# Modulation merged into the projection stage, and the slot table laid out partition by partition

## The chip, the cores and the metric

The kernel runs on one core of a Trainium2 chip, as one program with one launch. The metric is the device time of an execution in microseconds (us); the median of several runs counts.

## What is computed

One block of a transformer with adaptive LayerNorm: 8 batches of 1024 tokens, 512 wide. A small vector c per batch gives six rows (shift, scale and gate for each half of the block); the second half is a mixture of 32 experts with 4 experts chosen per token and room for 256 tokens each.

```python
mod = (_silu(L0_c) @ L0_wmod).reshape(L0_c.shape[0], 6, 1, -1)
sa, ca, ga, sb, cb, gb = (mod[:, 0], mod[:, 1], mod[:, 2], mod[:, 3], mod[:, 4], mod[:, 5])
ga = (2 * (ga >= 0) - 1) * jnp.maximum(jnp.abs(ga), 0.25)
gb = (2 * (gb >= 0) - 1) * jnp.maximum(jnp.abs(gb), 0.25)
h = _layernorm(x, axis=-1) * (1 + ca) + sa
x = x + ga * _L0_attn_ref(h, w_q, b_q, w_k, b_k, w_v, b_v, w_o, b_o)
h = _layernorm(x, axis=-1) * (1 + cb) + sb
x = x + gb * _L0_ffn_ref(h, gate_w, bias_corr, up_w, down_w, shared_up_w, shared_down_w)
...
pos = jnp.take_along_axis(jnp.cumsum(oh, axis=0) - 1, e_flat[:, None], axis=1)[:, 0]
valid = pos < CAP
xe = jnp.zeros((E, CAP, D), flat.dtype).at[e_flat, pos].set(flat[tok], mode='drop')
```

## The kernel before

The program is a row of five stages, each a block of its own: modulation, projection to Q, K and V, attention, the feed-forward stage (output projection, routing, shared expert), and the 32 experts. A stage begins when the one before has ended on all engines, its DMAs included. Within a stage the five engines run their own hand-written orders and meet by semaphores. Semaphores of most stages start with a credit of 16, which one engine (SP in the projection and the expert stage) gives by one increment each at the stage's start, ahead of its first DMA.

**Modulation** (lines 103 to 194) loads c and the six 1 MB parts of `wmod`, computes silu(c) on ScalarE and VectorE (DVE), multiplies with an 8-column stationary operand into six PSUM banks, makes `res` (8 rows by 6 by 512) on DVE and stores it to `mod_rows` in DRAM. An fp32 matmul shows as two records in the trace. SP also stores zeros as padding and the initial slot table: `slot_info` has 8192 slots of two numbers (token, weight). Slot = expert * 256 + place, and the table in SBUF is `info[p, n]` with slot = n * 128 + p, so that neighbours along a partition lie 1 KB apart in DRAM and each slot is a piece of 8 bytes.

**Projection** (`stage_qkv`) works in 16 units of 512 tokens (two halves of each batch). For a unit, DVE makes LayerNorm statistics and normalises (`layernorm`, L370 to L378), GpSimd multiplies by the scale row and adds the shift row (`modulate`, L311 and L313; both rows are loaded by SP as broadcasts of `mod_rows`), TensorE transposes into two PSUM banks `ps_t` (`turn`), and ScalarE and DVE split the result in a high and a low part (`turn`, `low_turned`). Then come 12 products of 12 matmuls each: n = 0 to 3 with the Q weights, 4 to 7 with K, 8 to 11 with V. Weights are split in high and low parts too (`high_weights` on ScalarE, L389 on DVE), in the opening. For n below 8 ScalarE takes `out_hi` and DVE `out_lo` (L400) from a ring of four buffers each, which come free when SP's stores have landed. The work of unit u + 1 up to its transposes lies inside unit u; transposes of k = 0 to 3 come after products 7 to 10. Every other unit, SP waits for GpSimd's `modulate` of the next unit, to reload the two rows, before it issues the unit's first store.

**Experts** load the slot table (`info`) and the gate rows gb, turn them to token numbers on DVE (L1680 on), gather tokens by them, and add each expert's result to the output with an indirect DMA. In the feed-forward stage GpSimd writes token and weight of every chosen pair into `slot_info` with 16 indirect DMAs of 128 entries per unit (L1140), at the index that DVE computes in `give_slots`.

Of the kernel before, what the change touches and what calls it, by code (L numbers as in the profile page):

```python
# [102 lines left out]
def stage_modulation(nc, cT, wmod, mod_dram, h2_dram, info_dram, out):  # L103


    with ExitStack() as ctx:
        s = Scope(nc, ctx, "mod_", credit=False)
        c_sb = s.sb("c", [P, DK, NB], FP32)
        sig = s.sb("sig", [P, DK, NB], FP32)
        silu = s.sb("silu", [P, DK, NB], FP32)  # L110
        w_sb = s.sb("w", [P, DK, 6 * D], FP32)
        res = s.sb("res", [NB, 6, D], FP32)
        sign = s.sb("sign", [NB, 2, D], FP32)
        mag = s.sb("mag", [NB, 2, D], FP32)
        ps = [s.ps(f"ps{j}", (NB, D)) for j in range(6)]
        SP_TILES = SLOTS // P
        zero = s.sb("zero", [P, D], FP32)
        pad_i = s.sb("pad_i", [P, SP_TILES], I32)
        info = s.sb("info", [P, SP_TILES, 2], FP32)
        pool_own = s.sem("pool_own")  # L120
        loaded, sig_done, silu_done = s.sem("loaded"), s.sem("sig"), s.sem("silu")
        mm, own, ready, stored = s.sem("mm"), s.sem("own"), s.sem("ready"), s.sem("stored")
        gates = (M_GA, M_GB)
        ORDER = gates + (M_SA, M_CA, M_SB, M_CB)
        w_in = s.sems("w_in", 2)
        block = ctx.enter_context(nc.Block())

        @block.sync
        def _(sp):
            sp.dma_start(c_sb[:, :, :], cT.rearrange("(k p) b -> p k b", p=P)).then_inc(loaded, 16)  # L130
            for n, j in enumerate(ORDER):
                cols = slice(j * D, (j + 1) * D)
                sp.dma_start(w_sb[:, :, cols], wmod[:, cols].rearrange("(k p) n -> p k n", p=P)).then_inc(w_in[n >= 2], 16)
            sp.wait_ge(pool_own, 2)
            for r in range(CAP // P):
                sp.dma_start(h2_dram[T + r * P:T + (r + 1) * P, :], zero[:, :]).then_inc(stored, 16)
                sp.dma_start(out[T + r * P:T + (r + 1) * P, :], zero[:, :]).then_inc(stored, 16)
            sp.dma_start(info_dram.rearrange("(n p) c -> p n c", p=P), info[:, :, :]).then_inc(stored, 16)
            sp.dma_start(mod_dram[NB:NB + 1, :, :].rearrange("b j d -> (b j) d"), zero[0:6, :]).then_inc(stored, 16)
            sp.wait_ge(ready, 1)  # L140
            sp.dma_start(mod_dram[0:NB, :, :], res[:, :, :]).then_inc(stored, 16)
            sp.wait_ge(stored, 16 * (2 * CAP // P + 3))

        @block.gpsimd
        def _(pool):
            pool.memset(zero[:, :], 0.0)
            pool.memset(info[:, :, :], 0.0)
            pool.iota(pad_i[:, :], pattern=[[0, NE], [P, CAP // P]], base=T, channel_multiplier=1).then_inc(pool_own, 1)
            pool.wait_ge(pool_own, 1)
            pool.tensor_copy(info[:, :, 0], pad_i[:, :]).then_inc(pool_own, 1)  # L150

        @block.scalar
        def _(act):
            act.wait_ge(loaded, 16)
            act.activation(sig[:, :, :], c_sb[:, :, :], ACT.Sigmoid).then_inc(sig_done, 1)

        @block.tensor
        def _(pe):
            pe.wait_ge(silu_done, 1)
            for n, j in enumerate(ORDER):  # L160
                pe.wait_ge(w_in[n >= 2], (64 if n >= 2 else 32))
                for k in range(DK):
                    last = pe.matmul(ps[j][:, :], silu[:, k, :], w_sb[:, k, j * D:(j + 1) * D],
                                     start=k == 0, stop=k == DK - 1)
                last.then_inc(mm, 1)

        @block.vector
        def _(dve):
            dve.wait_ge(sig_done, 1)
            dve.tensor_tensor(silu[:, :, :], c_sb[:, :, :], sig[:, :, :], ALU.mult).then_inc(silu_done, 1)  # L170
            for n, j in enumerate(gates):
                dve.wait_ge(mm, n + 1)
                last = dve.tensor_copy(res[:, j, :], ps[j][:, :])
            last.then_inc(own, 1)
            dve.wait_ge(own, 1)

            for n, j in enumerate(gates):
                dve.tensor_scalar(sign[:, n, :], res[:, j, :], 0.0, 2.0, ALU.is_ge, ALU.mult)
                last = dve.tensor_scalar(mag[:, n, :], res[:, j, :], -1.0, 0.25, ALU.mult, ALU.max)
            last.then_inc(own, 1)  # L180
            dve.wait_ge(own, 2)
            for n, j in enumerate(gates):
                last = dve.tensor_tensor(mag[:, n, :], mag[:, n, :], res[:, j, :], ALU.max)
            last.then_inc(own, 1)
            dve.wait_ge(own, 3)
            for n, j in enumerate(gates):
# [1645 lines left out]
```

## Time and profile before

| what | value |
|---|---|
| median of 3 runs | 3338.03 us (3325.95 to 3339.06) |
| the profiled execution, its own time | 3321.04 us |
| its span | 3319.3 us |
| mean granted TensorE clock | 0.954 of full |
| busy: PE, DVE, POOL, ACT | 91%, 65%, 57%, 42% |

PE is TensorE, PEld its weight loads, DVE VectorE, ACT ScalarE, POOL GpSimd, SP the engine that issues most DMAs; SPq is its queue, where the time beside a DMA is that of issuing it. Each row of a timeline gives start, length, engine, line of the kernel, operation, output and inputs, and in brackets how long the engine had been idle and what released it.

### The profile page before, as it was taken

The numbers are of one execution on the slowest core, as the hardware profiler recorded it, in microseconds if no ns is written. First come the engines' busy times: TensorE is split into PE (matmuls) and PEld (weight loads), VectorE is DVE, ScalarE is ACT, GpSimd is POOL, SyncE is SP. The second block draws the span as 40 slices with busy tenths as digits, with TensorE's granted clock in tenths as the row PEclk, the third lists the DMA queues.
The fourth block names the chain that finished last, engine by engine and source line by source line (L and its number), as shares of the span: only waits on it lengthen the run. The fifth ranks groups of instructions, "written<-read, shape, count | busy, mean of one in ns | idle before, by whom it ended". The sixth has DMA issues, their size and how long they took to land. (4 is left out here: it accounts for less than half of the span.)

```text
span 3319.3 us, 52119 instructions
## 1 busy us (share of the span) xinstructions
PE 3023.0 (91%) x16704; PEld 2188.1 (66%) x16704; DVE 2144.3 (65%) x5331; ACT 1384.5 (42%) x2755; POOL 1888.6 (57%) x1107
## 2 busy tenths in 40 slices
PE   3999999789999999999999669999999999966997
PEld 0888888655556556555656258777777777745776
DVE  3545555377767776777677257778777777735674
ACT  1212222136666666566666432332332233214674
POOL 2332332237777777777777525565664765653664
PEclk7999999979999999999999789999999999977998
DMA  8556555555445544554453323323323223107996
GB/s 163 172 173 209 180 199 174 160 123 129 111 105 127 131 105 105 129 129 104 111 129 79 100 81 111 102 67 98 114 67 98 89 92 92 60 13 214 236 241 132
DMA packets 297669, 419.49 MB, mean 126 GB/s; under 512 B 64776, under 2 KB 148744, under 8 KB 297495
## 3 DMA queue, kind: packets, MB, share of 16 engines
q1 hardware_dynamic: 274974, 383.70, 41.9%
q0 software_dynamic: 22528, 33.72, 5.2%
q8 instruction: 86, 1.41, 0.2%
q14 instruction: 81, 0.66, 0.1%
HBM read 262.85 MB, written 153.01 MB: 125 GB/s over the span
## 5 line engine op out<-in xcount | busy, mean ns | idle before, releaser
L677 POOL TENSOR_TENSOR att_pt<-att_pt 128x2048 f32<-128x2048 f32 (+3 forms) x286 | 892.2, 3120 | 319.2 <-PE att_ps_o L825 306.0
L718 ACT ACTIVATE att_pt<-att_ps_p 128x512 f32<-128x512 f32 (+3 forms) x1536 | 679.7, 496 | 491.8 <-PE att_ps_p L874 291.9
L751 DVE CUSTOM_DVE_ANT_0 att_ps_s<-att_ps_s,att_causal 128x512 f32<-128x512 f32 (+3 forms) x1024 | 492.8, 505 | 152.4 <-PE att_ps_s L815 148.8
L871 PE MATMUL att_ps_p<-att_qs,att_ks 98*128 98x512 f32 (+3 forms) x1536 | 555.3, 386 | 6.7 <-DMA att_qs<-att_m_lo 3.2
L815 PE MATMUL att_ps_s<-att_ks,att_qs 96*128 96x512 f32 (+3 forms) x1536 | 487.9, 375 | 22.7 <-DMA att_ks<-qk_parts 22.0
L871 PEld LDWEIGHTS att_ps_p<-att_qs,att_ks 98*128 98x128 f32 x1536 | 288.9, 190 | 280.3 <-ACT att_pt L718 172.9
L757 DVE TENSOR_REDUCE att_lower<-att_ps_s 128x1 f32<-128x512 f32 x512 | 352.0, 688 | 178.7 <-PE att_ps_s L815 176.9
L1140 POOL DMA_INDIRECT slot_info<-ffn_info,ffn_slot x256 | 272.8, 1065 | 123.9 <-issue 77.6
L815 PEld LDWEIGHTS att_ps_s<-att_ks,att_qs 96*128 96x128 f32 x1536 | 278.1, 194 | 76.0 <-issue 22.4
L825 PE MATMUL att_ps_o<-att_pt,att_vs 128*32 128x512 f32 (+3 forms) x3072 | 328.0, 499 | 0.0
L311 POOL TENSOR_TENSOR qkv_x<-qkv_x,qkv_mod 128x512 f32<-128x512 f32 x64 | 91.1, 1424 | 363.6 <-DVE qkv_x L378 363.6
L1104 POOL TENSOR_TENSOR ffn_h<-ffn_h,ffn_mod 128x512 f32<-128x512 f32 x48 | 75.1, 1564 | 301.9 <-DVE ffn_h L1258 301.9
L874 PE MATMUL att_ps_p<-att_mask_k,att_ident_r 128*128 128x128 f32 x1024 | 240.1, 238 | 0.0
L1422 PE MATMUL ffn_ps_m<-ffn_dn_hi,ffn_a_hi 128*128 128x512 f32 x512 | 210.1, 410 | 9.1 <-DVE ffn_a_lo L1383 6.1
L400 DVE SCALAR_TENSOR_TENSOR qkv_out_lo<-qkv_ps_m,qkv_bqk,qkv_out_hi 128x512 fp32r<-128x512 f32 x128 | 93.4, 746 | 178.3 <-ACT qkv_out_hi L355 178.3
L1422 PE MATMUL ffn_ps_m<-ffn_dn_hi,ffn_a_lo 128*128 128x512 f32 x512 | 204.7, 400 | 2.4 <-issue 2.4
L1422 PE MATMUL ffn_ps_m<-ffn_dn_lo,ffn_a_hi 128*128 128x512 f32 x512 | 205.2, 401 | 1.3 <-issue 1.2
L1422 PE MATMUL ffn_ps_m<-ffn_hT_hi,ffn_up_hi 128*128 128x512 f32 x512 | 202.3, 395 | 3.3 <-issue 3.2
L1422 PE MATMUL ffn_ps_m<-ffn_hT_lo,ffn_up_hi 128*128 128x512 f32 x512 | 200.4, 391 | 3.6 <-issue 3.6
L1422 PE MATMUL ffn_ps_m<-ffn_hT_hi,ffn_up_lo 128*128 128x512 f32 x512 | 200.6, 392 | 2.7 <-issue 2.6
L443 PE MATMUL qkv_ps_m<-qkv_hT_hi,qkv_w_hi 128*128 128x512 f32 x512 | 200.5, 392 | 1.5 <-DVE qkv_hT_lo L383 1.5
L443 PE MATMUL qkv_ps_m<-qkv_hT_lo,qkv_w_hi 128*128 128x512 f32 x512 | 200.2, 391 | 0.0
(263 smaller groups left out, 6229.3 us busy)
## 6 DMA issues: line engine op xcount, KB each, us to landing
att_qs<-qk_parts SPq DMA_DIRECT2D x96, 512.0 KB, 6.8
att_ks<-qk_parts SPq DMA_DIRECT2D x96, 512.0 KB, 13.2
qk_parts<-qkv_out_hi SPq DMA_DIRECT2D x128, 256.0 KB, 2.6
qk_parts<-qkv_out_lo SPq DMA_DIRECT2D x128, 256.0 KB, 2.9
qkv_x<-x SPq DMA_DIRECT2D x16, 1024.0 KB, 5.5
v_rows<-qkv_out_v SPq DMA_DIRECT2D x64, 256.0 KB, 2.3
att_vs<-v_rows SPq DMA_DIRECT2D x32, 512.0 KB, 16.0
o_parts<-att_o SPq DMA_DIRECT2D x64, 256.0 KB, 6.6
```

The source lines that it names most:

```text
L400: dve.scalar_tensor_tensor(out_lo[n % RING][:, :], ps_m[n % BANKS][:, :], bqk_sb[:, n:n + 1], raw(out_hi[n % RING][:, :]), op0=ALU.add, op ...
L443: last = pe.matmul(ps_m[n % BANKS][:, :], w_part[:, k, (n % NG) * P:(n % NG + 1) * P], h_part[:, k, :], start=k == 0 and a + c == 0, stop= ...
L677: pool.tensor_tensor(into, into, tile(c)[:, :, col:UNIT], ALU.add).then_inc(add_done, 1)
L718: act.activation(tile(c)[:, h, col:UNIT], ps_p[n % NP][:, col:UNIT], ACT.Exp, scale=float(HD) ** -0.5).then_inc(exp_done, 1)
L751: dve.tensor_tensor_reduce(bank, bank, causal[:, UNIT - (c1 - c0):UNIT], scale=1.0, scalar=MASKED, op0=ALU.add, op1=ALU.max, accum_out=row ...
L757: dve.reduce_max(lower[:, low:low + 1], bank, axis=AX.X).then_inc(max_done, 1)
L815: pe.matmul(ps_s[at % NS][:, 0:c1 - c0], qs[cur.slot][0:STACK, h, t * P:(t + 1) * P], ks[cur.slot][0:STACK, h, c0:c1], start=True, stop=Tr ...
L825: last = pe.matmul(ps_o[h * HD:(h + 1) * HD, col:UNIT], vs[group.slot][:, kt, h * HD:(h + 1) * HD], tile(c)[:, h, col:UNIT], start=kt == 0 ...
L871: last = pe.matmul(ps_p[n % NP][:, col:UNIT], ks[prev.slot][:, h, kt * P:(kt + 1) * P], qs[prev.slot][:, h, q0:(qh + 1) * UNIT], start=Tru ...
L874: last = pe.matmul(ps_p[n % NP][:, col:col + P], ident_r[:, :], mask_k[:, :], start=False, stop=True)
L1140: pool.indirect_dma_start(info_dram[:, :], bass.IndirectOffsetOnAxis(slot[half][:, j:j + 1].bitcast(U32), 0), info[half][:, j, :], None, b ...
L1422: last = pe.matmul(bank, a[m], c[n], start=i + j == 0, stop=i + 1 == len(pairs) and j == 2)
```

## The change

The modulation stage is gone and its work stands in `stage_modulate_qkv`. Batch 0 takes its scale and shift rows straight from PSUM: silu of its c is copied over 128 columns (`silu_first`), so that the product has the row in all 128 partitions, and DVE, not GpSimd, multiplies and adds in unit 0. The other rows come in three pairs (`PAIRS`), each product with 32 columns (`silu_lane`), two side by side in one PSUM bank, one pair in the opening, one after product 6 of unit 0, one after product 4 of unit 1. The gate pair has five DVE operations. Weights are split in another order: Q before the transposes, K and V after. The first two units are written out, ahead of the loop. Padding is stored from the projection stage.

The slot table's SBUF layout stays `info[p, n]`, but in DRAM slot = p * 64 + n, 512 bytes in a row for each partition, and `give_slots` computes that index. In the projection and the expert stage the credits are given by TensorE, not SP.

```diff
-def stage_qkv(nc, x, wqkvT, bqk, bv, mod_dram, qk_dram, v_dram):
+def stage_modulate_qkv(nc, x, cT, wmod, wqkvT, bqk, bv, mod_dram, qk_dram, v_dram, h2_dram, info_dram, out):
...
+        PAIRS = ((M_CA, M_SA), (M_GA, M_GB), (M_CB, M_SB))
...
+        PAIR_AT = (6, 4)
...
 # SP
+            sp.dma_start(c_sb[:, :, :], cT.rearrange("(k p) b -> p k b", p=P)).then_inc(c_in, 16)
             load_x(0, 0)
-            load_mod(0)
+            load_pair(0)
...
+            sp.wait_ge(pair_done, 1)
+            load_pair(1)
+            store_rows(0)
+            sp.wait_ge(pool_own, CREDIT + 4)
+            for r in range(CAP // P):
+                sp.dma_start(h2_dram[T + r * P:T + (r + 1) * P, :], zero[:, :]).then_inc(padded, 16)
+                sp.dma_start(out[T + r * P:T + (r + 1) * P, :], zero[:, :]).then_inc(padded, 16)
+            sp.dma_start(info_dram.rearrange("(p n) c -> p n c", p=P), info[:, :, :]).then_inc(padded, 16)
...
+                if isinstance(u, int) and u == 0:
+                    sp.wait_ge(pair_done, 2)
+                    load_pair(2)
+                    store_rows(1)
...
 # DVE
+            def take_pair(n, bank):
+                dve.wait_ge(pair_done, n + 1)
+                if n == 1:
+                    dve.tensor_copy(rows[n][:, :], bank)
+                    dve.drain()
+                    dve.tensor_scalar(sign[:, :], rows[n][:, :], 0.0, 2.0, ALU.is_ge, ALU.mult)
+                    dve.tensor_scalar(mag[:, :], rows[n][:, :], -1.0, 0.25, ALU.mult, ALU.max)
+                    dve.drain()
+                    dve.tensor_tensor(mag[:, :], mag[:, :], rows[n][:, :], ALU.max)
+                    dve.drain()
+                    dve.scalar_tensor_tensor(rows[n][:, :], sign[:, :], -1.0, mag[:, :], op0=ALU.add, op1=ALU.mult).then_inc(rows_done, 1)
+                else:
+                    dve.tensor_scalar_add(rows[n][0:LANE, :], bank[0:LANE, :], 1.0)
+                    dve.tensor_copy(rows[n][LANE:2 * LANE, :], bank[LANE:2 * LANE, :]).then_inc(rows_done, 1)
...
             layernorm(0, 0, 0)
-            for j in range(3):
+            dve.wait_ge(first_done, 1)
+            dve.tensor_scalar_add(mod[:, 1, :], ps_m[0][:, :], 1.0)
...
+                if isinstance(u, int) and u < 2 and n == PAIR_AT[u]:
+                    take_pair(u + 1, ps_t[1][0:2 * LANE, :])
...
 # TensorE
+            s.give_credit(pe)
+            def pair(n, bank):
+                for i in range(2):
+                    pe.wait_ge(wmod_in[i], 16 * (n + 1))
+                for k in range(DK):
+                    for i in range(2):
+                        last = pe.matmul(bank[i * LANE:(i + 1) * LANE, :], silu_lane[:, k, :, :].rearrange("p r b -> p (r b)"),
+                                         w_mod[:, k, i, :], start=k == 0, stop=k == DK - 1)
+                last.then_inc(pair_done, 1)
...
+                if isinstance(u, int) and 0 < u < 3 and k == 1:
+                    pe.wait_ge(rows_done, u + 1)
...
+                    if isinstance(u, int) and u < 2 and n == PAIR_AT[u]:
+                        pe.wait_ge(lo_done, CREDIT + DK * (u + 1))
+                        pair(u + 1, ps_t[1])
...
 # give_slots, feed-forward stage, DVE
-                dve.tensor_scalar(over[:, :, :], place[:, :, :], float(CAP), float(SLOTS), ALU.is_ge, ALU.mult)
-                dve.scalar_tensor_tensor(place[:, :, :], expert[:, :, :], float(CAP), place[:, :, :], op0=ALU.mult, op1=ALU.add)
+                dve.tensor_scalar(over[:, :, :], place[:, :, :], float(P), float(1 - SLOTS), ALU.is_ge, ALU.mult)
+                dve.scalar_tensor_tensor(place[:, :, :], expert[:, :, :], 1.0 / NE, place[:, :, :], op0=ALU.mult, op1=ALU.add)
                 dve.drain()
-                dve.tensor_tensor(slot[half][:, :].rearrange("p (t k) -> p t k", t=UT), place[:, :, :], over[:, :, :], ALU.add).then_inc(slot_done, 1)
+                dve.scalar_tensor_tensor(slot[half][:, :].rearrange("p (t k) -> p t k", t=UT), place[:, :, :], float(SLOTS // P),
+                                         over[:, :, :], op0=ALU.mult, op1=ALU.add).then_inc(slot_done, 1)
...
 # expert stage, SP (and s.give_credit(pe) at the head of TensorE's part)
-            s.give_credit(sp)
-            sp.dma_start(info[:, :, :], info_dram.rearrange("(n p) c -> p n c", p=P)).then_inc(consts, 16)
+            sp.dma_start(info[:, :, :], info_dram.rearrange("(p n) c -> p n c", p=P)).then_inc(consts, 16)
```

SP's queue, before: from the store of the slot table in the modulation stage to the weights in the projection stage (L259 is x of unit 0, L263 the two broadcast rows; ahead of this piece stand c, the six parts of `wmod` and the padding).

```order
L138 DMA slot_info<-mod_info 128x64x2
L139 DMA mod_rows<-mod_zero 6x512
L141 DMA mod_rows<-mod_res 8x3072
L106 UNCONDITIONAL_BRANCH
L254 UNCONDITIONAL_BRANCH
L259 DMA qkv_x<-x 128x4x512
L263 DMA qkv_mod<-mod_rows 128x512 x2
L268 DMA qkv_wraw<-wqkvT 128x4x512 x3
```

The same place now, from the first load to the first pair's rows; `qkv_w_mod` holds two parts of `wmod`, and there is no end of a stage in between.

```order
L200 DMA qkv_c<-cT 128x4x8
L185 DMA qkv_x<-x 128x4x512
L193 DMA qkv_w_mod<-wmod 128x4x512 x2
L204 DMA qkv_wraw<-wqkvT 128x4x512 x3
L205 DMA qkv_bqk<-bqk 128x8
L206 DMA qkv_bv<-bv 128x512
L185 DMA qkv_x<-x 128x4x512
L193 DMA qkv_w_mod<-wmod 128x4x512 x2
L198 DMA mod_rows<-qkv_rows 8x512 x2
```

x has moved ahead of all of `wmod` but c, four parts of `wmod` have moved behind the weights, and the slot table behind the first pair's rows.

DVE's opening of the projection stage, before, from the end of `inverse_root` of unit 0 on.

```order
L97 TENSOR_SCALAR qkv_tmp<-qkv_tmp 128x4
L99 TENSOR_TENSOR qkv_rstd<-qkv_rstd,qkv_tmp 128x4
L378 TENSOR_SCALAR qkv_x<-qkv_x,qkv_mv,qkv_rstd 128x512 x4
L389 TENSOR_TENSOR qkv_w_lo<-qkv_wraw,qkv_w_hi 128x2048 x3
L383 TENSOR_TENSOR qkv_hT_lo<-qkv_ps_t,qkv_hT_hi 128x512 x4
```

And now: `qkv_mod` are the rows in all partitions, L365 is the low part of a weight, L360 and L361 take a pair.

```order
L339 TENSOR_SCALAR qkv_x<-qkv_x,qkv_mv,qkv_rstd 128x512 x4
L374 TENSOR_SCALAR qkv_mod<-qkv_ps_m 128x512
L378 TENSOR_TENSOR qkv_x<-qkv_x,qkv_mod 128x512 x4
L365 TENSOR_TENSOR qkv_w_lo<-qkv_wraw,qkv_w_hi 128x2048
L381 COPY qkv_mod<-qkv_ps_m 128x512
L385 TENSOR_TENSOR qkv_x<-qkv_x,qkv_mod 128x512 x4
L344 TENSOR_TENSOR qkv_hT_lo<-qkv_ps_t,qkv_hT_hi 128x512 x4
L360 TENSOR_SCALAR qkv_rows<-qkv_ps_m 32x512
L361 COPY qkv_rows<-qkv_ps_m 32x512
L365 TENSOR_TENSOR qkv_w_lo<-qkv_wraw,qkv_w_hi 128x2048 x2
L331 BN_STATS qkv_stats<-qkv_x 128x6 x4
```

The multiplications and additions of unit 0 have come to DVE, one weight part stands between them, and two weight parts and the first pair's rows stand behind the transposes, ahead of the statistics of unit 1 (the last row).

DVE in unit 0 now, from the first seven low outputs on; before, the eighth `qkv_out_lo` followed the seventh at once.

```order
L399 SCALAR_TENSOR_TENSOR qkv_out_lo<-qkv_ps_m,qkv_bqk,qkv_out_hi 128x512 x7
L351 COPY qkv_rows<-qkv_ps_t 64x512
L353 TENSOR_SCALAR qkv_sign<-qkv_rows 64x512
L354 TENSOR_SCALAR qkv_mag<-qkv_rows 64x512
L356 TENSOR_TENSOR qkv_mag<-qkv_mag,qkv_rows 64x512
L358 SCALAR_TENSOR_TENSOR qkv_rows<-qkv_sign,qkv_mag 64x512
L399 SCALAR_TENSOR_TENSOR qkv_out_lo<-qkv_ps_m,qkv_bqk,qkv_out_hi 128x512
L344 TENSOR_TENSOR qkv_hT_lo<-qkv_ps_t,qkv_hT_hi 128x512
```

Five operations for the gate rows (L351 to L358) have come between the seventh and the eighth low output.

## Rows read from the trace of the kernel before

**Rows 1.** The page's busy times: engine, busy us (share), instructions.
```profile
PE 3023.0 (91%) x16704; PEld 2188.1 (66%) x16704; DVE 2144.3 (65%) x5331; ACT 1384.5 (42%) x2755; POOL 1888.6 (57%) x1107
```

**Rows 2.** The chain that ended last: start us, us, what.
```profile
3076.23 5.22 DMA out<-exp_y,exp_tok_add
```

**Rows 3.** Stretches: busy us of each engine, granted clock, DMA share, GB/s.
```profile
9.40:19.20 9.80, 9.71 (x16) 1.66 (x16) 0.68 (x1) 0.00 (x0) 0.00 (x0) 1.00 1.05 404
...
34.00:42.00 8.00, 0.00 (x0) 0.00 (x0) 0.24 (x1) 0.00 (x0) 0.00 (x0) 0.80 1.14 16
...
39.00:40.00 1.00, 0.00 (x0) 0.00 (x0) 0.00 (x0) 0.00 (x0) 0.00 (x0) 0.50 0.71 16
...
90.00:92.00 2.00, 2.00 (x10) 1.65 (x9) 2.00 (x2) 0.57 (x1) 1.92 (x2) 1.00 0.00 0
```

**Rows 4.** Timeline of the modulation stage: start us, us, engine, line, operation.
```profile
9.46 9.71 PE L163 MATMUL mod_ps<-mod_w,mod_silu 128*8 128x512 f32 x16 [9.46 <-DMA mod_w<-wmod]
...
14.12 21.64 SPq L139 DMA_DIRECT2D mod_rows<-mod_zero  x1
...
15.77 0.68 DVE L173 COPY mod_res<-mod_ps 8x512 f32<-8x512 f32 x1 [12.57 <-PE mod_ps L163]
...
19.62 13.90 PE L163 MATMUL mod_ps<-mod_w,mod_silu 128*8 128x512 f32 x32 [0.46 <-DMA mod_w<-wmod]
...
35.80 0.28 SPq L141 DMA_DIRECT2D mod_rows<-mod_res  x1
```

**Rows 5.** Who waited for whom, SP, 0 to 60 us: total, times, longest.
```profile
SPq L106 <- DMA mod_rows<-mod_res: 12.5, 1, 12.5
```

**Rows 6.** Timeline of the projection stage's opening.
```profile
56.17 2.47 DVE L370 BATCH_NORM_STATS2 qkv_stats<-qkv_x 128x6 f32<-128x512 f32 x4 [21.93 <-DMA qkv_x<-x]
...
60.82 3.82 DVE L378 TENSOR_SCALAR qkv_x<-qkv_x,qkv_mv,qkv_rstd 128x512 f32<-128x512 f32 x4
...
64.56 9.90 DVE L389 TENSOR_TENSOR qkv_w_lo<-qkv_wraw,qkv_w_hi 128x2048 fp32r<-128x2048 f32 x3
...
72.39 3.19 POOL L313 TENSOR_TENSOR qkv_x<-qkv_x,qkv_mod 128x512 f32<-128x512 f32 x1
...
78.23 1.94 PE L419 MATMUL qkv_ps_t<-qkv_ident,qkv_x 128*128 128x128 f32 x8 [44.71 <-POOL qkv_x L313]
...
84.26 0.79 PE L443 MATMUL qkv_ps_m<-qkv_hT_hi,qkv_w_hi 128*128 128x512 f32 x1 [1.50 <-DVE qkv_hT_lo L383]
```

**Rows 7.** Timeline of the expert stage's opening, and the DMA row of the load of c.
```profile
2999.08 0.20 POOL L199 MEMSET exp_ident<- 128x128 f32 x1 [10.85 <-POOLq L897]
...
3000.96 0.37 SPq L1586 DMA_DIRECT2D exp_info<-slot_info  x1
...
3007.59 0.20 DVE L1680 CAST exp_tok_all<-exp_info 128x64 int32<-128x64 f32 x1 [13.37 <-DMA exp_gb<-mod_rows]
...
3012.38 1.23 DVE L1711 TENSOR_TENSOR exp_up_lo<-exp_upr,exp_up_hi 128x1024 fp32r<-128x1024 f32 x1 [3.08 <-ACT exp_up_hi L1649]
...
mod_c<-cT SPq DMA_DIRECT2D x1, 16.0 KB, 1.9
```

**Rows 8.** Timeline of the projection stage's first unit (DVE, GpSimd, SP).
```profile
84.04 2.46 DVE L370 BATCH_NORM_STATS2 qkv_stats<-qkv_x 128x6 f32<-128x512 f32 x4
...
99.00 1.30 POOL L313 TENSOR_TENSOR qkv_x<-qkv_x,qkv_mod 128x512 f32<-128x512 f32 x1
...
101.67 0.37 SPq L287 DMA_DIRECT2D qk_parts<-qkv_out_hi  x1
...
107.21 0.75 DVE L400 SCALAR_TENSOR_TENSOR qkv_out_lo<-qkv_ps_m,qkv_bqk,qkv_out_hi 128x512 fp32r<-128x512 f32 x1 [7.57 <-ACT qkv_out_hi L355]
...
121.84 0.69 DVE L407 TENSOR_TENSOR qkv_out_v<-qkv_ps_m,qkv_bv 128x512 f32<-128x512 f32 x1 [1.45 <-PE qkv_ps_m L447]
```

**Rows 9.** The page's costliest groups: busy us, mean ns, idle before.
```profile
L825 PE MATMUL att_ps_o<-att_pt,att_vs 128*32 128x512 f32 (+3 forms) x3072 | 328.0, 499 | 0.0
```

**Rows 10.** Timeline of GpSimd in the feed-forward stage, after 16 scatters.
```profile
2635.30 1.50 POOL L1104 TENSOR_TENSOR ffn_h<-ffn_h,ffn_mod 128x512 f32<-128x512 f32 x1 [15.71 <-DVE ffn_h L1258]
```

More of the change, by code:

```diff
@@ L100, in inverse_root @@
     dve.wait_ge(own, base + 5)
[L103 to L186, printed above, removed]
-                dve.scalar_tensor_tensor(res[:, j, :], sign[:, n, :], -1.0, mag[:, n, :], op0=ALU.add, op1=ALU.mult)
-            for n, j in enumerate(ORDER[2:]):
-                dve.wait_ge(mm, n + 3)
-                if j in (M_CA, M_CB):
-                    last = dve.tensor_scalar_add(res[:, j, :], ps[j][:, :], 1.0)
-                else:
-                    last = dve.tensor_copy(res[:, j, :], ps[j][:, :])
-            last.then_inc(ready, 1)
@@ L229, in stage_qkv @@
         out_v = [s.sb(f"out_v{n}", [P, D], FP32) for n in range(UT)]
+        c_sb = s.sb("c", [P, DK, NB], FP32)
+        sig = s.sb("sig", [P, DK, NB], FP32)
+        silu = s.sb("silu", [P, DK, NB], FP32)
+        LANE = 32
+        silu_lane = s.sb("silu_lane", [P, DK, LANE // NB, NB], FP32)
+        silu_first = s.sb("silu_first", [P, DK, P], FP32)
+        PAIRS = ((M_CA, M_SA), (M_GA, M_GB), (M_CB, M_SB))
+        w_mod = s.sb("w_mod", [P, DK, 2, D], FP32)
+        rows = [s.sb(f"rows{n}", [2 * LANE, D], FP32) for n in range(3)]
+        sign, mag = s.sb("sign", [2 * LANE, D], FP32), s.sb("mag", [2 * LANE, D], FP32)
+        SP_TILES = SLOTS // P
+        zero = s.sb("zero", [P, D], FP32)
+        pad_i = s.sb("pad_i", [P, SP_TILES], I32)
+        info = s.sb("info", [P, SP_TILES, 2], FP32)
         ps_t = [s.ps(f"ps_t{n}") for n in range(2)]
         ps_m = [s.ps(f"ps_m{n}") for n in range(BANKS)]
+        c_in, sig_done, silu_done = (s.sem(n, False) for n in ("c_in", "sig", "silu"))
+        wmod_in, first_done, pair_done = s.sems("wmod_in", 2, False), s.sem("first", False), s.sem("pair", False)
+        rows_done, rows_out = s.sem("rows", False), s.sem("rows_out", False)
+        padded = s.sem("padded", False)
         w_in, w_hi_done, w_lo_done = s.sems("w_in", 3), s.sem("w_hi_done"), s.sem("w_lo_done")
@@ L246, in steps @@
         def steps(eng, body):
-            with eng.Fori(0, LAST) as b:
+            for half in range(HALVES):
+                body(0, half, True)
+            with eng.Fori(1, LAST) as b:
                 for half in range(HALVES):
@@ new lines, in _ @@
+            layernorm(0, 0, 0)
+            dve.wait_ge(first_done, 1)
+            dve.tensor_scalar_add(mod[:, 1, :], ps_m[0][:, :], 1.0)
+            dve.drain()
+            for t in range(UT):
+                xt = x_sb[0][:, t, :]
+                dve.tensor_tensor(xt, xt, mod[:, 1, :], ALU.mult).then_inc(mul_done, 1)
+            low_weights(0)
+            dve.wait_ge(first_done, 2)
+            dve.tensor_copy(mod[:, 0, :], ps_m[1][:, :])
+            dve.drain()
+            for t in range(UT):
+                xt = x_sb[0][:, t, :]
+                dve.tensor_tensor(xt, xt, mod[:, 0, :], ALU.add).then_inc(h_done, 1)
@@ L412, in _ @@
         def _(pe):
+            s.give_credit(pe)
[7 more added lines that the diff above has]
+                last.then_inc(pair_done, 1)
+            pe.wait_ge(silu_done, 1)
+            for i in range(2):
+                pe.wait_ge(wmod_in[i], 16)
+                for k in range(DK):
+                    last = pe.matmul(ps_m[i][:, :], silu_first[:, k, :], w_mod[:, k, i, :], start=k == 0, stop=k == DK - 1)
+                last.then_inc(first_done, 1)
+            pair(0, ps_m[2])
             pe.wait_ge(pool_own, CREDIT + 2)
@@ L972, in stage_project_route_shared @@
         LAST = NB - 1
+        assert CAP == 2 * P
         PT = UT - 1
```

50 lines of the change are left out of this document (41 added, 9 removed).

## The prediction

> **What bounds the kernel now.** I read the page first: TensorE is busy 91% of the span [rows 1], so time can be won only where it idles. The chain that ended last shows one such place: from 3076 us to the end it is a row of 28 scatter-adds, each waiting for the one before (the first stands in [rows 2]), so whatever starts the expert stage earlier ends the kernel earlier by as much. The stretches show the other place, the start. Between 34 and 42 us next to nothing runs on any engine, while the 16 DMA engines are full and move 16 GB/s [rows 3]. The timeline says with what: SP is stuck for 21.64 us behind the store of the 64 KB slot table, which is cut in 8-byte pieces, and can issue the store of the modulation rows only at 35.80 [rows 4]; SP then waits 12.5 us for that store [rows 5]. The projection stage starts only behind that, and its first projection matmul stands at 84.26 [rows 6]. The load of the slot table and of gb keeps the expert stage from 3000.96 to 3007.59 [rows 7].
>
> The profiled execution took 3321.0 us, 1.7 more than its span. It is the fastest seen; the runs give 3326 to 3339, median 3338.0. I sum against the execution and carry the difference over to the median.
>
> **The opening, step by step.** One block replaces two, so SP issues c, x, the first two wmod parts (scale, shift), then the three weights, on one queue. In front of the scale part stand as many bytes as in front of the second gate part now, so it lands when TensorE could start before, 9.46 [rows 4]. x lands one megabyte earlier, 2.6 us at the 404 GB/s these loads reach [rows 3], at 6.9; statistics and normalising take 60.82 + 3.82 - 56.17 = 8.5 [rows 6], so x is ready at 15.4. The scale product is four fp32 matmuls, as the first gate is now, whose copy starts at 15.77 [rows 4]. That ends last. DVE then has in order, with 0.7 for a 128x512 operation (the 0.69 of [rows 8]): scale from PSUM 0.7, four multiplications 2.8, the low part of the Q weights, the shift copy 0.7, four additions 2.8.
>
> The Q weights' low part takes 9.90 / 3 = 3.3 now [rows 6]; the 128x1024 form takes 1.23 [rows 7], so twice that, 2.5, is what it costs alone. I take 2.5, since GpSimd, whose own additions grow to 3.19 beside it [rows 6] against 1.30 later [rows 8], has nothing to do in the new opening. The Trainium skill (SBUF — State Buffer, "Who interferes with whom") says that a DVE instruction with two SBUF inputs contends with a GpSimd one that reads SBUF, and the trace agrees with 3.3 and 3.19 side by side. Without that rule the opening would come out 0.8 later and the first unit 1.7 more.
>
> So h is ready at 15.8 + 0.7 + 2.8 + 2.5 + 0.7 + 2.8 = 25.3. From the first transpose to the first projection matmul it is 84.26 - 78.23 = 6.0 [rows 6], so that matmul comes at 31.3 and not 84.26: **-53.0**. The shift product and the first pair end by 23 and hide behind DVE. Bounds: at the full clock the transposes take some 1 less and the first 12 matmuls 2.5 less; TensorE's granted clock had fallen to 0.50, the 1.2 GHz level, by 39, after its last modulation matmul at 33.5 [rows 3, 4], and was at 1.00, 2.4 GHz, from 90 on, 6 us into the projection [rows 3]. In the new order it idles only about 2 us before the transposes. I leave the clock as it was (sum: 0, or -3.5). The other way, loads later by 2 and the 3.3 above: +3.
>
> **What moves into the first two units.** The two pairs left are 16 matmul records each, 32 columns wide, two lanes. A record of 512 columns is 0.43 at 2.4 GHz (13.90 / 32, the second modulation burst [rows 4]), so one by one a pair costs 6.9. The attention's 32-column matmuls take 328.0 / 3072 = 0.107 each with four lanes [rows 9], so lanes do overlap; I take two at a time, **+3.5 twice**, with 6.9 twice as the other bound. The Trainium skill (TensorEngine Tiling (Array Packing), "Key Properties") states that tiles operate in parallel and that a change of tiling mode drains the array; the trace agrees on the first, and no row here prices the second.
>
> In unit 0 there is a new wait too. DVE makes two weight parts and a pair's rows after its low transposes, 1.4 + 2.5 + 2.5 = 6.4, so it starts the next LayerNorm 6.3 after the first matmul, where it starts 0.2 before it now [rows 8]. From there GpSimd needs 16.3 (99.00 + 1.30 - 84.04) and SP, whose stores are queued behind a wait for it, issues the first store 1.4 later; the fifth low output follows 5.5 after (107.21 - 101.67) [rows 8]. Counted from the first matmul: 6.3 + 16.3 + 1.4 + 5.5 = 29.5 instead of 22.9. The ring of four output buffers thus makes DVE's seventh low output end at 32.9, and only then come the gate rows in DVE's order, five operations of 0.4 to 0.7 with three drains, 3.0: done at 35.9. TensorE must not write that bank with the second transposes until then. It reaches them at 28.0 (now: 121.84 less three steps of 3.2, less 84.26) plus 3.5 = 31.5. So it waits **+4.4**; bounds 0 (if DVE catches up) and 8. Unit 1 has no such queue: SP there waits for no GpSimd, the last pair's load (2 MB) is issued 1.4 into the unit and lands by some 10, against a need at 13.7.
>
> The padding stores stand behind SP's prologue and nobody waits for them before the end of the stage: 0. In 512-byte pieces the slot table no longer fills the queue. The routing edit puts one DVE operation for another of the same size: 0.
>
> **The expert stage.** SP loses its credit increments, so its first load goes out at about 2999.1, when the stage's first instruction runs, and not at 3000.96, and the table arrives in 128 pieces. The other small load, c, took 1.9 to land [rows 7]; with some 0.5 for a second issue info and gb are there at about 3001.6, by when TensorE has given the credits: **-6.0**, bounds -4 and -6.5. Expert weights are issued earlier by the same amount, so nothing else takes the wait's place, and the chain behind shifts as a whole [rows 2].
>
> **Sum.** -53.0 + 3.5 + 3.5 + 4.4 - 6.0 = -47.6, that is 3273.4 for a profiled execution. The median of before less that is 3290.4. As the runs before spread over 13 us with the fastest at 3326, I put the median a little lower, at **3288**.
>
> **The rivals.**
> 1. *The opening comes, but half is given back in the first two units.* Lanes don't overlap (+7), the wait is 8 (+3.6), loads land later (+3), only 4 from the expert stage (+2): 3273.4 + 15.6 = 3289 profiled, 3304 as median. For it: TensorE is the bound there and each added microsecond counts. Against: [rows 9]. Chance 0.17.
> 2. *The full clock from the start*: -3.5, and no wait in unit 0 because the stores keep up, -4.4: 3280 as median. For it: the short idle. Against: the transposes from 78.23 on did not bring the clock up before the projection began [rows 3, 6]. Chance 0.15.
> 3. *The table was not what delayed the expert stage*: with the gb rows or the weights landing last, the 6.0 is lost and the median is 3294. Chance 0.08.
> 4. *Slower.* The new index puts the 128 entries of each of the 256 scatters 512 bytes apart instead of side by side within an expert. If each took d longer on GpSimd, its 16 scatters per unit first eat the idle 15.7 that it has before its next work [rows 10], 0.98 each; from there each microsecond lands on 15 units. To cancel 48 they must take 0.98 + 48 / (15 x 16) = 1.18 longer, more than double; 1.4 longer would give 3390. Against: GpSimd only makes 128 descriptors each time, as before, and the landings are waited for a whole unit later. Chance 0.02.
> 5. *Under 0.5% in all*: an unseen wait of 30 in the unrolled code or in the merged stage's queue, 3321. Chance 0.03.
>
> The forecast itself has 0.55, with a range of its own from 3276 to 3300. A difference of 0.5% (17 us) is about what a measurement of this kernel can tell from none. Rivals 1 to 3 and the forecast are all beyond it, 0.95; same 0.03; slower 0.02. The range for 8 in 10 takes in rivals 2 and 3 and most of 1: 3268 to 3304.
>
> **What the new profile would show.** The first transposes at about 25 and the first projection matmul at 31, no stretch with full DMA engines and no bytes; scale product's end at 15.8; three DVE weight parts of 2.5 and not 3.3; TensorE waiting near 63 to 67 us for DVE's gate rows; pair records at half their length apart; the third unit's first matmul some 42 us earlier than now; SP's info load issued with the stage's start, and the first DVE cast of tokens 2.5 after it. I am wrong if scatters take over 2 us each, if TensorE waits in unit 0 for over 8, or if the expert stage still opens on a wait of 5 or more.

## The result: 0.6% faster, where 1.5% was forecast

The changed kernel takes 3315.64 us (median of 22 runs, 3299.85 to 3339.43) beside 3335.68 for the kernel before (22 runs): ratio 0.9943, 95% interval 0.9925 to 0.9961. That is 20 us less, where the prediction had 50 less than its median of 3338, and it lies outside the range of 3268 to 3304. The profiled execution took 3308.46 us, 12.6 us less in span (3306.7 against 3319.3). One repeat of the changed kernel in the last group of runs below took 8454.88 us at a granted clock of 0.35 and is left out of that kernel's ratio.

First the page of the changed kernel, the busy row that answers to [rows 1].

```profile
span 3306.7 us, 51930 instructions
PE 3024.1 (91%) x16720; PEld 2188.0 (66%) x16720; DVE 2139.4 (65%) x5338; ACT 1384.9 (42%) x2755; POOL 1873.8 (57%) x1099
```

It does not tell where the missing 30 us went: TensorE's sum is 1 us larger than before. So I read the timeline at places that both kernels have. The opening, which answers to [rows 4] and [rows 6] (start us, us, engine, line, operation):

```profile
7.06 2.47 DVE L331 BATCH_NORM_STATS2 qkv_stats<-qkv_x 128x6 f32<-128x512 f32 x4 [3.17 <-DMA qkv_x<-x]
...
9.88 9.63 PE L429 MATMUL qkv_ps_m<-qkv_w_mod,qkv_silu_first 128*128 128x512 f32 x16 [9.88 <-DMA qkv_w_mod<-wmod]
...
16.12 0.69 DVE L374 TENSOR_SCALAR qkv_mod<-qkv_ps_m 128x512 f32<-128x512 f32 x1 [2.48 <-PE qkv_ps_m L429]
...
19.30 2.29 DVE L365 TENSOR_TENSOR qkv_w_lo<-qkv_wraw,qkv_w_hi 128x2048 fp32r<-128x2048 f32 x1
19.44 3.63 PE L421 MATMUL qkv_ps_m<-qkv_w_mod,qkv_silu_lane 128*32 128x512 f32 x16
...
24.86 1.06 PE L440 MATMUL qkv_ps_t<-qkv_ident,qkv_x 128*128 128x128 f32 x8 [1.79 <-issue]
...
29.63 0.50 PE L466 MATMUL qkv_ps_m<-qkv_hT_hi,qkv_w_hi 128*128 128x512 f32 x1 [1.41 <-DVE qkv_hT_lo L344]
```

Each step stands within half a microsecond of where the prediction put it, until the transposes, which run at a granted clock of 1.00: 1.06 us for the first eight where it was 1.94 [rows 6]. The expert stage's opening, which answers to [rows 7]:

```profile
2990.53 0.35 SPq L1613 DMA_DIRECT2D exp_info<-slot_info  x1
2990.53 0.21 POOL L105 MEMSET exp_ident<- 128x128 f32 x1 [10.05 <-POOLq L923]
...
2993.50 0.20 DVE L1707 CAST exp_tok_all<-exp_info 128x64 int32<-128x64 f32 x1 [7.77 <-DMA exp_gb<-mod_rows]
```

The load goes out with the stage's first instruction and the cast follows 2.97 later. Now the marks side by side, each a start time read from the timeline:

| mark | before | after | difference |
|---|---|---|---|
| fourth LayerNorm of the projection | 157.01 | 115.81 | -41.2 |
| feed-forward stage, first ffn_h of VectorE | 1923.55 | 1883.61 | -39.9 |
| expert stage, GpSimd's first instruction | 2999.08 | 2990.53 | -8.6 |
| first transpose of the expert stage | 3017.10 | 3003.51 | -13.6 |
| end of the span | 3319.3 | 3306.7 | -12.6 |

The opening's gain arrives at the feed-forward stage almost whole, and 31.4 of it is gone when that stage ends. The change alters three small operations in that stage, of the same sizes as before. Its units show the pattern: before the change, units follow each other in about 63.2 us; after it about every second one takes 69.6. The two windows are one such unit of each (busy us of PE, PEld, DVE, ACT, POOL with counts, granted clock, DMA share, GB/s), before and then after:

```profile
2571.70:2634.70 63.00, 60.52 (x283) 48.93 (x282) 48.82 (x103) 19.52 (x34) 40.26 (x34) 0.97 0.27 88
```

```profile
2143.10:2212.70 69.60, 61.32 (x275) 47.99 (x274) 47.96 (x103) 19.64 (x34) 39.25 (x34) 0.95 0.23 76
```

No engine has more work. TensorE's 61.32 us instead of 60.52 go with a granted clock of 0.95 instead of 0.97; the rest of the 6.6 us is waiting. VectorE's timeline of the changed kernel inside such a unit shows on what:

```profile
2168.05 0.18 DVE L1388 SCALAR_TENSOR_TENSOR ffn_slot<-ffn_place,ffn_over 128x16 int32<-128x16 f32 x1
2174.16 0.29 DVE L1407 TENSOR_TENSOR ffn_logits<-ffn_logits,ffn_ps_g 128x128 f32<-128x128 f32 x1 [5.93 <-issue]
...
2176.62 0.23 DVE L1311 TENSOR_TENSOR ffn_pair_hi<-ffn_biased 128x64 f32<-128x64 f32 x1 [1.37 <-issue]
```

L1388 is the last operation of the loop's body and L1407 the first: the 5.93 us lie across the jump back. L1311, a few operations on, waits a second time, 1.37 us; experiments e9 to e12 come back to it. "Issue" means that the engine waited for nothing that the profile shows: no semaphore, no buffer. What ended VectorE's idle time before that sum of logits, before the change and after it (us, times):

```profile
L1379 DVE TENSOR_TENSOR ffn_logits<-ffn_logits,ffn_ps_g x16: 286/289/291, 1948.8 to 2907.9; 128x128 f32<-128x128 f32 x16
...
  issue: 1.8, 5
```

```profile
L1407 DVE TENSOR_TENSOR ffn_logits<-ffn_logits,ffn_ps_g x16: 286/289/289, 1908.6 to 2899.7; 128x128 f32<-128x128 f32 x16
...
  issue: 30.4, 5
```

Five times 6 us, once for each jump back of a loop with six passes. The page's part on queues shows what went on meanwhile. These are the queues that load instructions (packets, MB, share), before and after.

```profile
q8 instruction: 86, 1.41, 0.2%
q14 instruction: 81, 0.66, 0.1%
```

```profile
q8 instruction: 89, 1.46, 0.2%
q14 instruction: 107, 0.88, 0.1%
```

26 more packets of 8 KB (0.88 MB in 107). By windows, 25 of them fall into 1880 to 3000 us. One pass of the loop after the change, from 2249 to 2382, has this row; the same window of the kernel before, 2251 to 2378, has none at all:

```profile
q14 instruction: 5, 0.04, 0.1%
```

Over all five passes behind a jump (2168.2 to 2839.2) the changed kernel has 25 packets on q14 and one on q8; the kernel before (2213.4 to 2849.4) has one on q8 and none on q14:

```profile
q14 instruction: 25, 0.20, 0.1%
q8 instruction: 1, 0.02, 0.0%
```

### The profile page after: what moved, and what is told of

Read it like the earlier page. It is cut to its first block and busy times, and to the rows that moved or that the text cites. A ratio compares the mean times of both kernels' runs of the same rounds, so it can differ in the third digit from the quotient of the medians.

```text
span 3306.7 us, 51930 instructions
## 1 busy us (share of the span) xinstructions
PE 3024.1 (91%) x16720; PEld 2188.0 (66%) x16720; DVE 2139.4 (65%) x5338; ACT 1384.9 (42%) x2755; POOL 1873.8 (57%) x1099
## 3 DMA queue, kind: packets, MB, share of 16 engines
q8 instruction: 89, 1.46, 0.2%
## 5 line engine op out<-in xcount | busy, mean ns | idle before, releaser
L1167 POOL DMA_INDIRECT slot_info<-ffn_info,ffn_slot x256 | 269.4, 1052 | 123.4 <-issue 77.3
L271 POOL TENSOR_TENSOR qkv_x<-qkv_x,qkv_mod 128x512 f32<-128x512 f32 x60 | 83.5, 1392 | 385.0 <-DVE qkv_x L339 385.0
L900 PEld LDWEIGHTS att_ps_p<-att_mask_k,att_ident_r 128*128 128x128 f32 x1024 | 196.3, 192 | 5.7
```

Source lines behind the costliest of these rows:

```text
L900: last = pe.matmul(ps_p[n % NP][:, col:col + P], ident_r[:, :], mask_k[:, :], start=False, stop=True)
L1167: pool.indirect_dma_start(info_dram[:, :], bass.IndirectOffsetOnAxis(slot[half][:, j:j + 1].bitcast(U32), 0), info[half][:, j, :], None, b ...
```

## Theories

**A: the code's place.** Counted in the built program, VectorE's loop of the feed-forward stage is some 349 instructions of 64 bytes (to within two). A packet of 8 KB is a block of 128 instructions, so the loop is 2.7 packets long. The merged opening is unrolled and puts 88 more instructions ahead of it: it began at 4482, 2 past a multiple of 128, and now at 4570, 90 past. The theory: if the loop touches 3 blocks they stay with the engine; if 4, each jump back fetches the code anew. **B: the scatter.** The table's new index makes something in the stage slower. **C: another engine's code**, ScalarE's (35 later) or TensorE's (711 later), sets the stall and VectorE only shows it.

The kernel before took a median of 3325, 3239 and 3305 us in the three groups of runs below (e1 to e5; e6, e3, e7, e8; e9 to e12), so kernels are compared within a group.

## Experiments

### e1_pad40: VectorE's loop 40 instructions later

```diff
         def _(dve):
+            for _ in range(40):
+                dve.drain()
             dve.wait_ge(iotas, CREDIT + 1)
```

> The changed kernel with 40 drains ahead of VectorE's first wait of the feed-forward stage, where it stands idle 7.22 us for a load. Counted in the built program, VectorE's loop of that stage is 349 instructions of 64 bytes and begins at instruction 4482 before the change and at 4570 after it (88 later); in blocks of 128 (the 8 KB of an instruction packet) it touched 3 blocks before and touches 4 after. The drains put it at 4610, where it touches 3 again. Theory A (each jump back to the loop's start makes VectorE's code be fetched anew when it touches 4 blocks): instruction packets of the 8 KB queue fall from 107 to about 83, the feed-forward stage from 995 us back to 963, the whole by about 31, to a profiled time near 3277 and 0.982 to 0.986 of the kernel before. Theory B (the new slots' scatter holds up the stage): no change, 3308, 0.994. Theory C (it is the code of ScalarE or TensorE that moved): no change, 3308.

A drain computes nothing. The 40 of them stand in front of the stage's first wait and delay nothing: the first ffn_h starts at 1883.52 with them and at 1883.61 without.

Measured: 3280.63 us against 3324.57 before, ratio 0.9852 (0.9807 to 0.9897). Packets and VectorE's idle time before the sum of logits:

```profile
q14 instruction: 82, 0.67, 0.1%
```

```profile
L1409 DVE TENSOR_TENSOR ffn_logits<-ffn_logits,ffn_ps_g x16: 286/289/289, 1909.2 to 2873.2; 128x128 f32<-128x128 f32 x16
...
  issue: 1.6, 5
```

And the stage as a window, from its first ffn_h to its last, without the drains and with them:

```profile
1883.61:2882.00 998.39, 916.38 (x4179) 729.65 (x4180) 713.99 (x1476) 298.49 (x515) 571.90 (x482) 0.96 0.28 88
```

```profile
1883.52:2855.48 971.96, 907.05 (x4179) 728.68 (x4180) 715.78 (x1476) 298.15 (x515) 575.63 (x482) 0.97 0.29 90
```

The 40 drains take 26.4 us off the stage. TensorE, too, is busy 9 us less for the same matmuls: its granted clock over the stage is 0.97 and was 0.96. B and C predicted no change and are out as the main cause.

### e2_before88: the same stall put into the kernel before

```diff
         def _(dve):
+            for _ in range(88):
+                dve.drain()
             dve.wait_ge(iotas, CREDIT + 1)
```

> The kernel before with 88 drains at the same place and nothing else, so that VectorE's loop of the feed-forward stage begins at 4570, as in the changed kernel. Theory A: slower by about 31 us (1.009 of the kernel before), some 24 more 8 KB instruction packets, all of it in the feed-forward stage, with idle times of about 6 us ahead of VectorE's sum of logits in five iterations. Theories B and C: no change but for what the drains themselves take beyond the idle time (under 1 us).

Measured: 3354.05 us, ratio 1.0085 (1.0052 to 1.0118): 29.5 slower, with nothing of the change in it.

```profile
q14 instruction: 106, 0.87, 0.1%
```

```profile
L1381 DVE TENSOR_TENSOR ffn_logits<-ffn_logits,ffn_ps_g x16: 286/288/290, 1944.5 to 2938.8; 128x128 f32<-128x128 f32 x16
...
  issue: 29.9, 5
```

25 more packets than the kernel before and the same five stops. A loss of the size of the changed kernel's (31.4) follows from the place of the code alone.

### e4_act93 and e5_old_table: ScalarE's code, and the table

```diff
+            for _ in range(93):
+                act.drain()
             high_weights(0, NW_UP)
```

> The changed kernel with 93 drains ahead of ScalarE's first wait of the feed-forward stage (idle 17.64 us there), so that ScalarE's loop stands 128 instructions after its place in the kernel before, that is the same within a block. Theory C for ScalarE: the stage falls to 963 us and the time to near 3277. Theory A: no change, 3308, and 107 instruction packets as before.

Measured: 3307.11 us (one run), 107 packets, five stops with 30.2 us. C for ScalarE is out. TensorE's code had no run of its own, but in e1 and e2 it stayed where it was while the stall went and came, and q8, the queue whose bytes fit TensorE's code, loads one packet in the five passes with the stall and one without.

```diff
-            sp.dma_start(info[:, :, :], info_dram.rearrange("(p n) c -> p n c", p=P)).then_inc(consts, 16)
+            sp.dma_start(info[:, :, :], info_dram.rearrange("(n p) c -> p n c", p=P)).then_inc(consts, 16)
...
-                dve.tensor_scalar(over[:, :, :], place[:, :, :], float(P), float(1 - SLOTS), ALU.is_ge, ALU.mult)
-                dve.scalar_tensor_tensor(place[:, :, :], expert[:, :, :], 1.0 / NE, place[:, :, :], op0=ALU.mult, op1=ALU.add)
+                dve.tensor_scalar(over[:, :, :], place[:, :, :], float(CAP), float(SLOTS), ALU.is_ge, ALU.mult)
+                dve.scalar_tensor_tensor(place[:, :, :], expert[:, :, :], float(CAP), place[:, :, :], op0=ALU.mult, op1=ALU.add)
```

The padding's store and the last line of the index go back in the same way.

> The changed kernel with the slot table and the scatter's index as before the change; the merged opening stays and VectorE's count of instructions is the same. Theory B (the scatter's new addresses hold up the feed-forward stage): the stage falls from 995 us towards 963, the time to about 3277 plus the 6 to 11 us that the expert stage's opening gives back. Theory A: the stage stays at 995, and the expert stage's opening gives back its 6 to 11 us, so 3314 to 3320.

Measured: 3325.71 us (one run), 107 packets: the stall stays, so B is out. Against the changed kernel's 3306.7 the span is 17.2 longer, and the loss is not where I expected most of it. SP's timeline in the merged opening, with the old table and then with the new:

```profile
33.23 0.46 SPq L215 DMA_DIRECT2D slot_info<-qkv_info  x1
33.73 16.23 SPq L216 DMA_DIRECT2D mod_rows<-qkv_zero  x1
50.01 1.37 SPq L185 DMA_DIRECT2D qkv_x<-x  x1
```

```profile
34.66 0.46 SPq L215 DMA_DIRECT2D slot_info<-qkv_info  x1
35.16 0.36 SPq L216 DMA_DIRECT2D mod_rows<-qkv_zero  x1
35.57 0.39 SPq L185 DMA_DIRECT2D qkv_x<-x  x1
```

The store in 8-byte pieces holds SP for 16.23 us, now in the middle of the first unit, whose outputs wait behind it: the fourth LayerNorm comes at 124.78 and not 115.81, +9.0. In the expert stage the cast of the tokens comes 7.1 after GpSimd's first instruction (3006.84 to 3013.98) and not 2.97, +4.2. The remaining 4 us lie in the feed-forward stage and at the end; it is one execution, and no cause is shown for them.

### e6_table_only: the second part of the change alone

```diff
-            sp.dma_start(info_dram.rearrange("(n p) c -> p n c", p=P), info[:, :, :]).then_inc(stored, 16)
+            sp.dma_start(info_dram.rearrange("(p n) c -> p n c", p=P), info[:, :, :]).then_inc(stored, 16)
...
-                dve.tensor_scalar(over[:, :, :], place[:, :, :], float(CAP), float(SLOTS), ALU.is_ge, ALU.mult)
+                dve.tensor_scalar(over[:, :, :], place[:, :, :], float(P), float(1 - SLOTS), ALU.is_ge, ALU.mult)
```

> The kernel before with the second part of the change alone: the slot table laid out partition by partition and the index to match; the modulation stage stays. VectorE's loop stays at 4482, so theory A expects no loss in the feed-forward stage (967 us). The store of the padding table (8 B pieces, behind which SyncE's next issue took 21.64 us and whose stage ended at about 50 us) no longer holds the stage up: some 12 us less; the expert stage's opening, from its load of the table to its first transpose, takes 12.5 to 13 us and not 16.1. Sum about -15, ratio near 0.9955. If the table's layout were worth nothing ahead of the merged opening, -3.5 alone, 0.999.

Measured: 3225.56 us against 3239.45, ratio 0.9955 (0.9941 to 0.9968); the first projection matmul at 72.72 where it was 84.26 [rows 6]. 80 packets, no stops. So the table alone is worth 14 us in the old order and, by the one run of e5, some 13 to 17 in the new.

### e3_pad128, e7_pad64, e8_pad84: is it the drains or the place?

```diff
-            for _ in range(40):
+            for _ in range(128):
                 dve.drain()
```

With 64 and 84 in the other two.

> The changed kernel with 128 drains at the same place as the 40 that gave 27 us back: VectorE's loop stands at 4698, one block of 128 later than in the changed kernel, and touches 4 blocks again. Theory A: 107 instruction packets on the 8 KB queue and the feed-forward stage at about 998 us, 3307 to 3310 in all. Rival (the drains themselves, or their pause, are what helps): about 3281.

> 64 drains: the loop is at instructions 4634 to 4981, in blocks 36 to 38, so 3 blocks. Theory A with blocks of 128 counted from the program's start: 82 instruction packets, stage near 972 us, time near 3281.

> 84 drains: the loop is at instructions 4654 to 5001, in blocks 36 to 39, so 4 blocks, with 20 more instructions ahead of it than with 64. Theory A: 105 to 107 packets, stage near 998 us, time near 3308.

Measured, with 3239.45 for the kernel before and one run each: 3220.31 us and 108 packets with 128 drains, 3214.94 and 107 with 64, 3210.89 and 108 with 84. All three stall, five times 6.1 to 6.2 us. Packets and stops came out as expected for 128 and 84 drains; the times that were expected were those of the first group. 64 was expected to be free of the stall and is not, so blocks counted from the program's own first instruction are wrong. The control matters most: 128 drains move the code by one whole block, and cure nothing. In this group a pass of the loop (two units) took 118.5 us without a stall (e6) and 122.4 to 123.7 with it (mean of five), so the same 6 us of VectorE cost 4 to 5; in the two profiles of the result it took 127.2 before the change and 134.2 after it, 7 more.

### e9_after_again, e10_pad40_again, e11_pad24, e12_pad52: the limits, and the better kernel

e9 is the changed kernel and e10 is e1, both unaltered; e11 and e12 have 24 and 52 drains.

```diff
-            for _ in range(40):
+            for _ in range(24):
                 dve.drain()
```

> The changed kernel, unaltered, beside the next three on one chip, since the runs with 64, 84 and 128 drains came from a session in which the kernel before took 3239 us and not 3325. Theory A: 107 instruction packets, ratio to the kernel before 0.991 to 0.995, five idle times of about 6 us ahead of VectorE's sum of logits.

> The 40 drains again, now beside the changed kernel: 82 packets, none of the five idle times, and faster than the changed kernel by the whole of what they cost, 20 to 31 us by the session: ratio to the kernel before 0.984 to 0.988.

> 24 drains: the loop at 4594 to 4941. The runs so far bear theory A out but not the count from the program's start: 4482 and 4610 (2 past a multiple of 128) let the loop stay, 4570 and 4698 (90 past), 4654 (46 past) and 4634 (26 past) don't. A loop of 349 stays within 3 blocks from 36 starts of 128, so something of 10 to 33 instructions must stand ahead of the program in the chip. 4594 is 114 past (14 short of the next multiple): it stays if that is 14 or more (82 packets), and does not if it is 10 to 13 (107).

> 52 drains: the loop at 4622, 14 past a multiple of 128. By the same count it stays (82 packets, no idle times) if 10 to 21 instructions stand ahead of the program, and does not (107) if it is 22 to 33. If it is the drains' own time and not the place that counts, it is as good as with 40.

| kernel | loop starts at | past 128 | packets | stops' sum, us | time (before 3304.70) |
|---|---|---|---|---|---|
| e9, no drains | 4570 | 90 | 107 | 30.7 | 3290.91, 0.9946 (0.9927 to 0.9965) |
| e11, 24 | 4594 | 114 | 82 | 1.7 | 3246.84 (one run) |
| e10, 40 | 4610 | 2 | 83 | 1.6 | 3249.73, 0.9830 (0.9804 to 0.9856) |
| e12, 52 | 4622 | 14 | 107 | 31.6 | 3276.89 (one run) |

The twelve drains between e10 and e12 bring the five stops back, those between e11 and e10 don't matter. With a loop of 349 that must lie within 3 blocks of 128, starts 114 and 2 are good and 14, 26, 46 and 90 bad only if 22 to 33 instructions stand ahead of the program on the chip.

The start times of the packets, read from the trace, show the blocks in another way. In e12 the pass behind the jump at 2419.4 loads packets at 2423.8, 2426.3, 2451.9, 2499.3 and 2548.8. Packets in 2419.5 to 2430, 2430 to 2465, 2465 to 2510 and 2545 to 2551:

```profile
q14 instruction: 2, 0.02, 0.5%
...
q14 instruction: 1, 0.01, 0.1%
...
q14 instruction: 1, 0.01, 0.1%
...
q14 instruction: 1, 0.01, 0.3%
```

Two come at the jump. The other three come when 84, 216 and 342 of VectorE's instructions of the pass have started, which is 98, 102 and 100 past a multiple of 128; in e7 it is 99, 101 and 96. So a block ends near there, which puts some 26 to 32 instructions ahead of the program, and on entering a block the engine loads the one behind it. That explains the count: a loop that touches 4 blocks also loads a fifth, which it never runs, and one that touches 3 loads a fourth. Four blocks stay and five do not. This is inferred from the packets' times; no row shows what the engine holds.

The second, small wait in the changed kernel fits this too. From a start at 90 only a dozen instructions are left in the first block, and L1311 behind them waits 6.4 us in all, six times; in e12 and e7, which start at 14 and 26, it does not wait.

The 40 drains beat the kernel before in both of their groups and the changed kernel in the one where both were timed. There they are 1.2 points below it, 41 us, more than the 31 of VectorE's stops. The five passes behind a jump show why, as windows of the kernel before and after, of e10 and e9, and of e6 and e7 (another kernel each, but the same feed-forward stage), each time without and with the stall (columns as in the windows above):

```profile
2213.40:2849.40 636.00, 604.77 (x2823) 486.32 (x2822) 484.08 (x1021) 195.70 (x340) 403.83 (x340) 0.99 0.29 91
2168.20:2839.20 671.00, 618.48 (x2821) 490.31 (x2820) 481.64 (x1021) 196.12 (x340) 398.64 (x340) 0.97 0.28 86
...
2164.90:2789.00 624.10, 602.53 (x2822) 485.17 (x2821) 484.81 (x1021) 196.03 (x340) 402.23 (x340) 0.99 0.30 93
2179.20:2840.20 661.00, 617.21 (x2822) 489.82 (x2821) 481.66 (x1021) 196.20 (x340) 395.76 (x340) 0.97 0.28 88
...
2189.40:2782.00 592.60, 592.60 (x2822) 481.62 (x2821) 485.58 (x1021) 195.21 (x340) 402.99 (x340) 1.00 0.31 98
2158.70:2773.00 614.30, 602.57 (x2822) 486.64 (x2821) 483.73 (x1021) 195.74 (x340) 399.03 (x340) 0.99 0.30 94
```

With the stops of 30 us TensorE idles 21, 22 and 12 us longer (window less its busy time), and the same matmuls take 14, 15 and 10 us longer. The granted clock reads 0.50, the 1.2 GHz level, for 44, 41 and 17 us of these windows, and for 17, 14 and 0 us without the stall. One such place in the changed kernel: TensorE idles 4.0 of 7.4 us, and then the clock is down:

```profile
2315.00:2322.40 7.40, 3.43 (x13) 2.13 (x12) 3.70 (x18) 1.64 (x3) 5.57 (x7) 1.00 0.02 0
2322.40:2329.10 6.70, 5.57 (x12) 3.75 (x12) 3.75 (x9) 3.45 (x7) 0.32 (x1) 0.50 0.00 0
```

Other pairs give less: 24 us between e4 and e1 (668.8 and 645.3), 26 between e12 and e10 (649.9 and 624.1). What sets the cost within 22 to 37 us is not shown. Of the 55 us between the spans of e9 and e10 (3303.8 and 3248.8) the passes are 37. Another 14 lie before the first jump, where there is no stop: e9's profiled execution is the slowest but one of its ten, and no cause is shown for them.

## Why the prediction was wrong, step by step

- **Opening, -53.0: right.** The first projection matmul is at 29.63, forecast 31.3, so -54.6. x's statistics from 7.06 (6.9), the scale copy from 16.12 (15.8), the low part of Q 2.29 long (2.5). Most of the 1.7 between forecast and measurement is the clock that I left as it was: TensorE's granted clock read 1.00 from 28 to 30, so rival 2 was right in this half. Its other half, no wait in unit 0, did not come.
- **Pairs, +3.5 twice: right.** A pair's 16 records take 3.63, where the prediction has 6.9 for one by one; the lanes overlap.
- **New wait in unit 0, +4.4: right in mechanism, 6.16 in size**, with the elements in the order named: the fifth low output 28.7 after the first matmul (29.5), and TensorE waiting for the gate rows from 58.7 on (forecast 63 to 67):

```profile
64.83 1.09 PE L440 MATMUL qkv_ps_t<-qkv_ident,qkv_x 128*128 128x128 f32 x4 [6.16 <-DVE qkv_rows L358]
```

  The wait ends 35.2 after the first matmul (forecast 35.9); TensorE reaches it at 29.0 and not 31.5. So what the full clock gains in the first matmuls becomes waiting. Behind the wait the granted clock reads 0.50 until 69.6.

- The sum of these was -41.6 in the forecast and is **-41.2** at the fourth LayerNorm (-54.6 + 3.6 + 3.6 + 6.2).
- **Expert stage, -6.0: nearly right.** From GpSimd's first instruction to the cast 2.97 and not 8.51, -5.5; to the first transpose 12.98 and not 18.02, -5.0. Of that, 1.0 is lost again by the end of the span.
- **The failed step** is the one that was not worked out: the sum took everything between the projection and the expert stage as shifted whole, and the routing edit in it at 0. That stretch lost 31.4, in the feed-forward stage: VectorE's code is fetched anew at five jumps back, five stops of 6 us (30.4 in all, 1.8 before), and TensorE idles and runs at the lower clock for it. The edits were costed by what their instructions do, and never by where they push the instructions behind them. Rival 5 had "an unseen wait of 30 in the unrolled code", with 3 in 100 and no mechanism. It was the size, but the stall was neither in the unrolled code nor in SP's queue: it is in a loop some 2,000 us later that kept its length.
- **Rival 4** is refuted: the scatters take 1052 ns on the mean and took 1065.

With the loop moved back the same sum holds: e1 lies 43.9 below the kernel before, forecast 47.6.

The prediction could have seen the risk. The profile of before has 81 packets of 8 KB, none of them inside the five passes of the feed-forward loop; the built program's count puts that loop at 349 instructions, and only about one start in four leaves such a loop within 3 blocks. The place was lucky before, and the change spent that luck. The Trainium skill (Runtime: NRT & Kernel Launch, "Instruction fetch mechanics") bears on it: most engines hold 32 KiB of instructions, and a taken branch whose target is not in what is held forces a fetch before execution can go on. The stops at the jump agree with the rule. The block size that it states, 16 KiB, is not what the packets of VectorE's code show, 0.88 MB in 107; it is that of the other instruction queue, 1.46 MB in 89. In blocks of 8 KB the 32 KiB of the Trainium skill would be four, by estimate, which agrees with the count of four that stay and five that do not.

## What to carry to other kernels

Code added ahead of a loop is a change to that loop. Before costing an edit that adds or removes instructions on an engine, count them, note each later loop's length and start in blocks of an instruction packet, and see whether it still lies in as many blocks as before (here a block ended some 96 to 102 instructions past a multiple of 128, counted from the program's start); afterwards compare the instruction queue's packets on the two pages, since a difference that first loading cannot explain is a loop being fetched anew. An idle time "issue" at the first operation of a body was its mark here, and drains in an idle place ahead of the loop are a cheap test and, in the right number, a cheap cure: 24 and 40 cured it; 52, 64, 84 and 128 did not.
